# Subtracting the row maxima from two key tiles and both heads at once, with four matmuls of 32 rows

## What is computed

```python
q = jnp.einsum('bsd,hdk->bhsk', x, w_q)
k = jnp.einsum('bsd,hdk->bhsk', x, w_k)
v = jnp.einsum('bsd,hdk->bhsk', x, w_v)
scores = jnp.einsum('bhqk,bhmk->bhqm', q, k) * scale
weights = jax.nn.softmax(scores, axis=-1)
z = jnp.einsum('bhqm,bhmk->bhqk', weights, v)
...
x = _layernorm(x + _L0_attn_ref(x, ...), axis=-1)
x = _layernorm(x + _L0_ffn_ref(x, ...), axis=-1)
```

## Time and profile before

| | |
|---|---|
| median of 3 runs | 1157.18 us (1154.05 to 1157.69) |
| the profiled execution, its own time | 1155.28 us |
| its span, first to last instruction | 1153.5 us |
| PE busy | 1061.5 us (92%) |
| DVE busy | 852.7 us (74%) |
| POOL busy | 727.1 us (63%) |
| ACT busy | 575.0 us (50%) |
| DMA, mean busy share of the 16 engines | 12.9% |

### The profile page before, as it was taken

How to read it: one execution, slowest core, us unless ns; L and a number is a source line. 1 busy time by engine, 2 the same in 40 slices (tenths; PEclk the granted TensorE clock), 3 DMA queues, 4 the chain that set the end, 5 groups by cost and what they waited for, 6 DMA issues and landing times. The chain is left out here.

```text
span 1153.5 us, 18564 instructions
## 1 busy us (share of the span) xinstructions
PE 1061.5 (92%) x5912; PEld 647.3 (56%) x5912; DVE 852.7 (74%) x1172; ACT 575.0 (50%) x680; POOL 727.1 (63%) x376
## 2 busy tenths in 40 slices
PE   4999899999999999999999999999957888889886
PEld 2555445555555555555555555556525666667664
DVE  4786778778878877877877887787735677776774
ACT  4554445455455454545545545444414565665563
POOL 0486656676666666667667666766745655666665
PEclk8899999999999999999999999999988899999999
DMA  7203012111111111111211111111000000000000
GB/s 182 78 20 110 19 42 78 46 45 59 45 45 61 62 45 45 59 45 45 77 45 45 59 46 45 50 73 46 33 27 10 10 19 12 8 18 18 9 10 19
DMA packets 41326, 52.31 MB, mean 45 GB/s; under 512 B 9296, under 2 KB 27728, under 8 KB 41296
## 3 DMA queue, kind: packets, MB, share of 16 engines
q1 hardware_dynamic: 41296, 51.92, 12.9%
HBM read 6.30 MB, written 2.10 MB: 7 GB/s over the span
## 5 line engine op out<-in xcount | busy, mean ns | idle before, releaser
L976 DVE TENSOR_REDUCE neg_max<-psum 128x2 fp32r<-128x1024 f32 x256 | 310.7, 1214 | 69.5 <-PE psum L507 67.0
L537 PE MATMUL psum<-q_pair,k_pair 64*128 64x512 f32 x1536 | 221.7, 393 | 3.3 <-DVE xT L958 1.9
L402 POOL TENSOR_TENSOR k_pair<-x_tok,q_pair 128x1024 fp32r<-128x1024 f32 x64 | 152.2, 2388 | 91.2 <-ACT q_pair L919 91.2
L367 POOL TENSOR_TENSOR probs_sum<-probs_sum,x_tok 128x1024 f32<-128x1024 f32 x64 | 152.6, 2384 | 72.3 <-ACT x_tok L824 69.3
L367 POOL TENSOR_TENSOR probs_sum<-probs_sum,probs_even 128x1024 f32<-128x1024 f32 x64 | 152.8, 2387 | 70.0 <-ACT probs_even L824 66.3
L824 ACT ACTIVATE probs_even<-psum 128x1024 f32<-128x1024 f32 x128 | 127.9, 1024 | 112.4 <-PE psum L543 112.4
L824 ACT ACTIVATE x_tok<-psum 128x1024 f32<-128x1024 f32 x128 | 128.3, 1025 | 110.1 <-PE psum L543 110.1
L537 PEld LDWEIGHTS psum<-q_pair,k_pair 64*128 64x128 f32 x1536 | 145.7, 186 | 32.5 <-DVE xT L958 2.4
L1175 DVE TENSOR_TENSOR x_tok<-x_tok,psum 128x1024 f32<-128x1024 f32 x64 | 77.9, 1217 | 78.2 <-PE psum L700 48.6
L555 PE MATMUL psum<-x_tok,v 128*64 128x512 f32 x512 | 132.5, 628 | 0.0
L555 PE MATMUL psum<-probs_even,v 128*64 128x512 f32 x512 | 128.4, 611 | 0.0
(11 more groups left out here) (117 smaller groups left out, 1836.7 us busy)
## 6 DMA issues: line engine op xcount, KB each, us to landing
xT_cur<-xT SPq DMA_DIRECT2D x32, 512.0 KB, 2.9
wqk_cur<-w_tab SPq DMA_DIRECT2D x62, 256.0 KB, 2.6
wo_cur<-w_tab SPq DMA_DIRECT2D x64, 128.0 KB, 2.0
x_tok<-L_attn_x_dram SPq DMA_DIRECT2D x8, 256.0 KB, 5.2
probs_even<-acc SPq DMA_DIRECT2D x8, 256.0 KB, 2.3
out_dram<-probs_even SPq DMA_DIRECT2D x8, 256.0 KB, 2.3
acc<-L_ffn_w_dram SPq DMA_DIRECT2D x1, 1024.0 KB, 5.7
acc<-L_attn_w_q_dram SPq DMA_DIRECT2D x1, 512.0 KB, 5.1
```

Of the source, the lines that this page charges most:

```text
L367: nc.gpsimd.tensor_tensor(probs_sum[:], left, probs[j][:, :, c, :], ALU.add).then_inc(s["added"], 1)
L402: nc.gpsimd.tensor_tensor(g_lo[e % GB], gated[e % 2], bits(g_hi[e % GB]), ALU.subtract).then_inc(s["g_lo_done"], 1)
L537: nc.tensor.matmul(psum[:, 2 * (t % 2) + h, :], k_pair[u][half, kp, keys], q_pair[u][half, qp, :], start=(kp == 0 and qp == 0), stop=False)
L976: nc.vector.tensor_reduce(neg_max[:].rearrange("p (h k) -> p h k", h=2)[:, :, t], psum[:, COARSE:COARSE + 2, :], AX.X, ALU.max, negate=Tru ...
```

## The change

The maxima are subtracted once for two key tiles, after the six products of both, by four matmuls instead of twice two: one for each tile g of the two and each head h, which contract over 32 rows each, rows h\*64+g\*32 to h\*64+g\*32+31. Each writes its own bank. For that the negated maxima must stand in both halves of a head's 64 rows:

- The mask gets a one in rows 0+t, 32+t, 64+t and 96+t (two more affine_select instructions on POOL at the start).
- A new DVE instruction in each body, **repeat_maxima** (line 989 of the changed file), copies the four columns of each head in `neg_max` to the columns 32 further on, after maxima 3. It waits for `max_done` of DVE itself. turn_maxima now waits for its semaphore `max_twice`, not for `max_done`.
- **subtract_max(n, t)** with t = 0 and t = 2 is called after scores 1 and after scores 3. `scores_done` rises by two at its end, and exps 0 and exps 1 (exps 2 and exps 3) wait for the same value.

```diff
             def turn_maxima(n):
-                pe.wait_ge(s["max_done"], TT * (n + 1))
+                pe.wait_ge(s["max_twice"], n + 1)
...
+            def subtract_max(n, t):
                 if t == 0:
                     pe.wait_ge(s["shift_done"], n + 1)
-                for h in range(2):
-                    half = slice(h * DK, (h + 1) * DK)
-                    mm = nc.tensor.matmul(psum[:, 2 * (t % 2) + h, :], ones_r[half, :],
-                                          shift[half].rearrange("p t q -> p (t q)"), start=False, stop=True)
-                mm.then_inc(s["scores_done"], 1)
+                for g in range(2):
+                    for h in range(2):
+                        rows = slice(h * DK + g * BLK, h * DK + (g + 1) * BLK)
+                        mm = nc.tensor.matmul(psum[:, 2 * g + h, :], ones_r[rows, :],
+                                              shift[rows].rearrange("p t q -> p (t q)"), start=False, stop=True)
+                mm.then_inc(s["scores_done"], 2)
...
                 scores(n, u, 0)
                 scores(n, u, 1)
+                subtract_max(n, 0)
...
                 scores(n, u, 2)
                 scores(n, u, 3)
+                subtract_max(n, 2)
...
-                act.wait_ge(s["scores_done"], TT * n + t + 1)
+                act.wait_ge(s["scores_done"], TT * n + t // 2 * 2 + 2)
...
+            def repeat_maxima(n):
+                dve.wait_ge(s["max_done"], TT * (n + 1))
+                columns = neg_max[:].rearrange("p (h g k) -> p h g k", h=2, g=2)
+                nc.vector.tensor_reduce(columns[:, :, 1, 0:TT], bits(columns[:, :, 0, 0:TT]).unsqueeze(3), AX.X,
+                                        ALU.max).then_inc(s["max_twice"], 1)
...
                     maxima(n + 1, 2)
                     maxima(n + 1, 3)
+                    repeat_maxima(n + 1)
```

More of the change, by code:

```diff
@@ L162, in attention_moe_kernel @@
             q_done k_done vT_done q_hi_done q_lo_done k_hi_done k_lo_done v_done
-            coarse_done max_cleared group_set max_done maxT_done mask_set shift_done
+            coarse_done max_cleared group_set max_done max_twice maxT_done mask_set shift_done
             scores_done exp_done added group_summed pv_done sums_done sums_out z_done r_done
@@ L352, in _ @@
             nc.gpsimd.memset(shift_mask[:], 0.0).then_inc(s["mask_set"], 1)
-            for i, first in enumerate((0, DK)):
+            for i, first in enumerate(range(0, P, BLK)):
                 pool.wait_ge(s["mask_set"], i + 1)
@@ L981, in shift_part @@
                 if is_first(n):
-                    dve.wait_ge(s["mask_set"], 3)
+                    dve.wait_ge(s["mask_set"], 5)
                 wait(dve, s["scores_done"], TT * n)
@@ L1035, in _ @@
                 maxima(0, t)
+            repeat_maxima(0)
             shift_part(0)
```

## The result

The changed kernel takes 1184.09 us (median of 4 runs, 1183.33 to 1184.31) where the kernel before takes 1156.33: the ratio is 1.0241, with a 95% interval of 1.0222 to 1.026. The change costs 28 us. The forecast was 15 us, in a range that reached to 1189. Its direction and its mechanism held; some 11 us of the loss came from a wait that it had costed at nothing and from the first bodies, which it had costed like the rest.

The account below looks back on a forecast made before the run. PE was taken to bound the loop, busy 199.25 of 200 us, with DVE next. Shape changes 0.21 plus scores 2's 0.03 gave 0.24 us per body, times 64 bodies +15 us: 1172 us, range 1151 to 1189.

Parts of the forecast that it names:

- The price of a group: PE, each group of four 32-row matmuls: two shape changes against two saved pitches, +0.17 us net.
- (b): PE's change from 64 rows to 32 and back: priced like 64 to 128, so the group costs 0.43 us.
- (a): The group's four matmuls on PE run at once, 0.23 us together; 0.46 if two went at a time.
- The gain of 3.07 for four: Skill's figure for four 32-row matmuls; by it the group streams 0.30 us, not 0.23, 9 us more in all.
- The first half half paid by acc_part's wait: Before project_q on PE: a hidden 0.13 us wait for acc_part absorbs most of the loss, leaving +0.04.
- The 2.65: Earliest start of project_q in a body, in us, set by acc_part's end on DVE whatever PE does before.
- The chain over q_part to maxima 2: ACT and DVE: later exps 0 delays q_part, reciprocals and maxima 2; coarse 3 still not held, margin gone.
- The 0.03 for scores 2: PE's scores 2 waits for later reciprocals to empty a bank: 0 to 0.09 us per body, 0.03 taken.
- Project_v: PE's third step behind coarse 3, at 9.05; exps 2 ends near 8.97, ahead of it, so cost nothing.
- 64 x 0.24: All 64 bodies costed alike at 0.21 + 0.03 us each, giving +15 us.
- The forecast's own bounds: With the two small terms' bounds, 0.19 to 0.30 us per body: 1169 to 1177 us.
- the rival of weights in two steps: Group's weights load in two steps on PE: 0.11 us per group, 14 us on top, 1186; chance half of 0.12.

Follow-up runs that it names:

- 32rows_each: Kernel before, subtraction in its old places by two matmuls per tile, but each over 32 rows of its head: 1244.34 us, ratio 1.0771.
- first_half: Changed kernel, but tiles 2 and 3 keep a subtraction of their own over 64 rows: 1161.76 us, ratio 1.0058.
- before_half_acc: Kernel before, with acc_part in the loop adding only half of its columns: 1149.04 us, ratio 0.9944.
- late64: Changed kernel with the subtraction still behind both tiles, but by twice two matmuls of 64 rows: 1180.57 us, ratio 1.0228.
- after_short: Changed kernel with exps 2 of the loop's even bodies doing one head only: 1178.14 us, ratio 1.0204.

## Why the prediction was right, and where it was short

- **The price of a group: right.** Forecast 1.83, 2.26 and 2.69 for the group, coarse 1 and project_q; 1.82, 2.25 and 2.68 in the trace. Second half: 7.39, 7.82 and 8.25 against 7.41, 7.85 and 8.28. Both unknown terms were taken rightly: (b) the price of the nearest row, which 32rows_each showed by itself, and (a) the four at once, since the group of four takes no longer than the group of two there. The rule of the Trainium skill, "TensorEngine Tiling (Array Packing)", Key Properties, that a change of the tiling mode drains the engine agrees with the 0.43 of the group between 64-row neighbours. The gain of 3.07 for four from "TensorE: Matmul & The Clock Gate" in the Trainium skill, Measured speedup vs the span model, does not show here: by the prediction's estimate from it the group would take 0.50, and a group of four (0.43) is as long as one of two (0.43).
- **The first half half paid by acc_part's wait: right,** 0.04 + 0.03 forecast, 0.08 in the odd bodies of first_half, and the wait is acc_part's (before_half_acc). The 2.65 is no fixed floor, though. In the bodies whose number is a multiple of four, project_q came at 2.55 in the kernel before already, and in late64; the prediction had read one odd body. So project_q moved by 0.08 in the even bodies in the mean (2.60 to 2.68) and by 0.02 in the odd ones (2.66 to 2.68), where 0.04 was forecast.
- **The chain over q_part to maxima 2: right,** a little too dear. q_part on ACT came at 4.20 (4.30 forecast), DVE's at 4.84 (4.90 to 5.0), maxima 2 ended at 7.55 (7.65 to 7.75), and coarse 3 showed no wait. The 0.03 for scores 2 shows too, not at its start but within it: from its start to the group it takes 1.52 in the mean, and the same stretch of the first half 1.48.
- **Project_v: the step that failed.** The forecast set the end of exps 2 (8.97) against the start of project_v (9.05) and costed it at nothing. The times were right to 0.02 on ACT, but 0.19 or 0.30 passes from the end on ACT to the load on PE, and PE, once held, has no weights loaded ahead. The term is 0.26 per even body of the loop, 7 us in all (6 of them won back in after_short).
- **The first nine bodies: mis-sized.** 64 x 0.24 counts 2.2 us for them; they lost 6.6. Body 0 lost 1.27, and only 0.17 of it by project_q. In both kernels its first half runs at a granted clock of 1.2 GHz, and in the changed kernel this lasts longer, as the windows from 38 to 42 us show, first before, then changed (columns as above):

```profile
38.00:42.00 4.00, 3.75 (x24) 2.14 (x22) 2.48 (x3) 1.65 (x3) 2.91 (x2) 0.88 0.01 3
...
38.00:42.00 4.00, 4.00 (x15) 2.75 (x17) 2.97 (x3) 1.74 (x3) 2.37 (x1) 0.50 0.05 16
```

  The clock rose to 2.4 GHz just before 39 us in the kernel before and at about 42.7 in the changed one, so there the products of tiles 2 and 3 ran at the lower level. In the nine traces without a group of 32 rows in the first half of a body it rose between 38.0 and 40.2, in the five with one between 41.8 and 44.8: it goes with the change, but no run took it apart. Body 6 lost 0.97. Two doublings stand there on ACT between exps 0 and exps 1 and wait for POOL, which comes to it 0.7 later behind the later add_probs, and scores 2 waits 1.83 for the reciprocals and not 1.27. The forecast had costed the later add_probs at nothing. In body 7 the clock stood at 1.2 GHz for 6.8 us and not 3.4, and in body 8 coarse 1 came 0.6 later, behind maxima 0. These causes are read from the traces and not tested.
- **Adding terms up was the wrong form.** In the even bodies the price of the shape and that of the late release overlap: 0.59 for the release alone (late64), 0.29 for the shape without the wait (after_short), 0.55 for both. Taking away the change of shape alone wins nothing there, and taking away the wait wins 0.26.
- **That 1184 lies in the range: luck in part.** The forecast's own bounds ended at 1177. The range reached up to 1189 for the rival of weights in two steps, at 1186, and that is not what happened: the four loads lie within 0.19, and the group takes 0.43 where two steps would have made it 0.54.

With the two missed terms, 15 + 7 + 4 is 26 of the 28 us.

## What to carry to other kernels

A pair of small matmuls that shares its neighbours' shape costs one pitch; put into a shape of its own it costs that pitch and 0.20 for each change, so saving one pitch of 0.23 by two changes did not pay: 0.17 lost for each group. Batching work so that its consumer starts later has a price even where a count of busy time shows slack: follow the consumer's end to the instruction that waits for it, and allow for the signal (0.19 to 0.30 from ACT to PE here) and for what the waiting engine could not load ahead (0.10). Where two such prices meet at the same wait, measure them one at a time in both orders before adding them.

## What the runs showed of the hardware

- PE's change between 32 and 64 rows costs 0.40 in and out together, for two matmuls in the group or four, the same as between 64 and 128 rows.
- Four matmuls of 32 rows to four banks take no longer than two: a group between changes of shape takes 0.43 with either, and the four weight loads lie within 0.19.
- A PE held for exps 2 pays twice: 0.19 or 0.30, by the body's place in the loop of four, from the end on ACT to the weight load, and about 0.1 until loads are ahead of matmuls again.
- After a wait of 2.46 us with PE idle, the granted clock of the next stretch was 0.66 in the mean, between the levels of 1.2 and 2.4 GHz; with a wait of 0.36 it stayed at 1.00.
